# First stage of a spectral attention kernel: GpSimd normalises tokens before it multiplies the attention's column weights, and the DMA queue follows

## The chip, the cores and the metric

The kernel runs on one core of a Trainium2 chip. The metric is the time of one execution in microseconds (us). Three runs of the kernel before took 486.02, 487.41 and 488.27 us; the median is 487.41 us. Five engines work side by side and meet through semaphores: TensorE (PE) multiplies matrices, VectorE (DVE), ScalarE (ACT) and GpSimd (POOL) work on tiles in on-chip memory, and SyncE (SP) mostly issues transfers (DMAs). ACT and POOL can issue transfers from their own queues too.

## The reference, cut to what matters

The input x is 4 x 32 tokens, each an image of 128 x 128. The layer first normalises each image row (`_ln_c`), then runs an attention whose key, query, value and projection are spectral convolutions with 16 heads, then a two-layer spectral mixer, and last a recurrent network over the rows.

```python
x = x + conv(_ln_c(x), ...)          # rows of 128 values: mean 0, variance 1
t = _to_tokens(x)
t = t + ffn(_ln_t(t), W, V, gamma, beta)

# inside conv
k = fno_layer(tokens_norm, key_w, key_skip_w, ...)       # spectral, 16 heads
q = fno_layer(tokens_norm, query_w, query_skip_w, ...)
v = fno_layer(tokens_norm, value_w, value_skip_w, ...)
dprod = softmax(einsum('bhtd,bhsd->bhts', q, k) / scale)
attn = einsum('bhts,bhsd->bhtd', dprod, v)
attn = fno_layer(attn, proj_w, proj_skip_w, ...)         # value and projection
```

Value and projection act on the same spectral modes. The kernel multiplies their weights once into one table `wy` (16 heads x 16 columns x 3 parts x 32 rows of modes) and applies it to the tokens' spectra.

## The kernel before, in words

The first stage works on `x_h` (the tile BIG2), which holds image rows on the partitions and 128 tokens of 128 values along the free side. It is loaded in XC = 8 chunks of 16 tokens. For each chunk

- DVE takes the moments (`ln_moments`, line 1156, 16 instructions and four small ones), asks ACT for a square root (line 942), and forms scale and shift (`ln_coefs`, lines 1175 and 1176; semaphore `ln_coef`);
- POOL normalises the first LN_POOL[c] tokens (line 566) and ACT the rest (line 979), in place;
- PE multiplies each normalised token with a Fourier basis (line 620), four tokens to a PSUM bank, in the order P1_AT: ACT's tokens of the chunk first, then POOL's;
- ACT moves the banks to `rs` in the tile BIG1 (`spectra`, line 389), one chunk behind its own normalising;
- SP writes the normalised chunk to DRAM (`xn_rows`, line 480), since its place in BIG2 is used again.

LN_POOL is 4, 8 and then six times 12, which makes 84 tokens for POOL and 44 for ACT. PE also multiplies `rs` with itself (`gram`), in pieces of work between the chunks 2 to 5 and after the stage.

Before it normalises, POOL copies four weight planes (line 534, waited for by PE's first transposes) and forms `wy` in 15 instructions (lines 551 to 561), the first of which waits for ACT's two instructions of line 968 (`wy_skip`). ACT runs those behind its queue of 27 small loads (lines 958 to 965). SP writes `wy` to DRAM (line 483) and reads it back as `wr`, each head's row repeated on 32 partitions: 16 transfers of 192 KB (line 489). They are spread between the writes of chunks 4 to 7 by WR_AFTER, and land in the first 6144 columns of BIG2, which chunks 0 to 2 held.

After the stage, PE forms inner products over the spectra (`rx`, eight banks moved by ACT and DVE), and the modes `ts` of every token. SP repeats `ts` as `xrep` on the partitions (line 496, 16 transfers of 192 KB, tile to tile), loads the mixer's weights (line 500) and reads the normalised tokens back from DRAM in another layout, `x_t` (line 511). `x_t` lies in BIG1 over `rs`, so its transfers 0 and 1 wait for the first of four grams, 2 and 3 for the second, and so on; the last two wait for the fourth. DVE forms the scores and the softmax and then multiplies `xrep` with `wr` (`products`, line 1262, 32 instructions: two, then the softmax's normalising, then six, then 8 and 16). The first two wait for all 16 transfers of `wr` (`rep_w`) and for the first half of `xrep`, the next six for its second half (`rep_x_23`). PE applies the attention to the products (`attend`), between pieces of gram. The mixer begins when `x_t` is there.

The order on each engine and in each queue is that of the code; nothing is planned at run time.

Of the kernel before, what the change touches and what calls it, by code (L numbers as in the profile page):

```python
# [149 lines left out]
def metaformer(nc, t, out):  # L150
# [4 lines left out]
    with ctx:  # L155
# [366 lines left out]
        def _(pool):  # L522
# [13 lines left out]

            def lows(v):
                return v.rearrange("n w (q h) -> n w q h", h=8)[:, :, 0::3, :]

            def a(part):  # L540
                return w_val[:, :, 1:9, part].rearrange("n (k h) w -> n w k h", k=2)

            def b(part):
                return lows(w_proj[:, :, 1:1 + LW, part].rearrange("n h w -> n w h"))


            pool.wait_ge(S("wy_skip"), 1)
            for part, (p, q, op) in ((0, (0, 0, ALU.add)), (0, (1, 1, ALU.subtract)),
                                     (1, (0, 1, ALU.add)), (1, (1, 0, ALU.add))):
                o = lows(wy[:, 0:LW, 1 + part, :])  # L550
                link(pool.tensor_tensor(wtmp, b(p), a(q), ALU.mult))
                link(pool.tensor_tensor(o, o, wtmp, op))
            for part in range(2):
                o = lows(wy[:, 0:LW, 1 + part, :])
                link(pool.tensor_scalar(wtmp, a(part), ps, None, ALU.mult))
                link(pool.tensor_tensor(o, o, wtmp, ALU.add))

            wy_re, wy_im = wy[:, :, 1, :], wy[:, :, 2, :]
            link(pool.tensor_tensor(wy[:, :, 0, :], wy_re, wy_im, ALU.add))
# [987 lines left out]
```

## Time and profile before

| what | value |
|---|---|
| median of three runs | 487.41 us |
| span of the profiled execution | 486.8 us |
| PE busy | 359.3 us (74%) |
| DVE busy | 349.1 us (72%) |
| ACT busy | 263.1 us (54%) |
| POOL busy | 232.1 us (48%) |
| mean granted clock of PE | 0.904 |
| bytes moved by DMA | 50.93 MB, 105 GB/s on average |

The profiled execution's own time is its span; 0.6 us lie between it and the median. The busy shares are averages over stages that have different limits, so the stage that the change touches, the first 140 us, has to be read by itself: in the chain of waits (what the end depended on, followed back), in the order of time on each engine, and in stretches of time with the transfer rates.

### The profile page before, as it was taken

How to read it: one execution, taken by the hardware profiler on the slowest of the kernel's cores; microseconds unless marked ns; L12 is line 12 of the kernel's file. 1: busy time of each engine (PE TensorE's matmuls, PEld its weight loads, DVE VectorE, ACT ScalarE, POOL GpSimd, SP SyncE). 2: the span in 40 equal slices, each digit the busy share in tenths (PEclk: the TensorE clock that was granted, in tenths of full speed). 3: DMA queues.
4: the chain of work that ended last, by engine and by line, in shares of the span. 5: the costliest groups of instructions: out<-in, count | busy, mean ns of one | idle time of the engine just before them, and what ended most of it. 6: DMA issues, size and time to landing. Idle time of an engine off the chain costs nothing.

```text
span 486.8 us, 7018 instructions
## 1 busy us (share of the span) xinstructions
PE 359.3 (74%) x2385; PEld 280.4 (58%) x2385; DVE 349.1 (72%) x954; ACT 263.1 (54%) x530; POOL 232.1 (48%) x268
## 2 busy tenths in 40 slices
PE   0169989998949999999916748666775557996790
PEld 0169967784529998799915724233332244664790
DVE  3689312798969645999586577777887369799790
ACT  0778743520227963555312147888889858597000
POOL 1499950000039949986111957666660599000000
PEclk9989999999969998999966957999989959799795
DMA  8999894998130007979980000000000000000599
GB/s 211 266 302 304 224 305 124 205 294 373 41 133 1 1 1 88 130 92 175 111 100 2 1 0 1 2 0 0 1 1 0 1 0 0 1 2 0 146 286 260
DMA packets 60692, 50.93 MB, mean 105 GB/s; under 512 B 4512, under 2 KB 54096, under 8 KB 59632
## 3 DMA queue, kind: packets, MB, share of 16 engines
q1 hardware_dynamic: 40928, 41.79, 29.4%
q0 software_dynamic: 16512, 8.39, 14.1%
q10 hardware_dynamic: 3216, 0.30, 0.6%
q8 instruction: 19, 0.31, 0.3%
q14 instruction: 17, 0.14, 0.1%
HBM read 30.45 MB, written 16.88 MB: 97 GB/s over the span
## 4 chain that ended last, share of the span: by engine, by line
DVE 38%; PE 27%; POOL 14%; ACT 9%; issue 5%; ACTq 3%; DMA 1%; DVEq 0%; SPq 0%
PE PS L620 24%; POOL BIG L566 8%; DVE PS L1468 7%; DVE BIG L1262 4%; DVE SML L1156 4%; PE PS L624 3%; DVE BIG L1436 3%; POOL BIG L606 3%; ACT BIG L1083 2%; POOL BIG L601 2%; DVE BIG L1519 2%; ACT SML L389 2%; DVE SML L1450 2%; ACTq L965 2%; DMA BIG<-xn_rows 1%
## 5 line engine op out<-in xcount | busy, mean ns | idle before, releaser
L620 PE MATMUL PS<-CST,BIG 128*128 128x128 f32 (+6 forms) x994 | 130.5, 327 | 22.6 <-ACT BIG L979 9.9
L620 PEld LDWEIGHTS PS<-CST,BIG 128*128 128x128 f32 (+1 forms) x994 | 115.4, 203 | 41.8 <-issue 13.7
L624 PE MATMUL PS<-CST,BIG 128*128 128x128 f32 (+1 forms) x326 | 53.9, 313 | 52.2 <-ACT SML L389 24.3
L624 PEld LDWEIGHTS PS<-CST,BIG 128*128 128x128 f32 (+1 forms) x326 | 43.9, 187 | 73.9 <-issue 54.6
L579 POOL COPY BIG<-BIG 128x512 f32<-128x512 f32 x24 | 30.2, 1307 | 74.8 <-DMA BIG<-xn_rows 71.2
L1156 DVE BATCH_NORM_STATS2 SML<-BIG 128x6 f32<-128x128 f32 x256 | 53.4, 279 | 6.1 <-DMA BIG<-in_x 4.8
L620 PE MATMUL PS<-BIG 128*128 128x128 f32 (+2 forms) x450 | 53.5, 368 | 2.6 <-DVE BIG L1262 2.1
L601 POOL TENSOR_TENSOR BIG<-BIG,SML 128x512 f32<-128x512 f32 x32 | 33.2, 1038 | 45.7 <-DVE SML L1176 27.9
L620 PE MATMUL PS<-BIG,SML 128*128 128x256 f32 (+3 forms) x214 | 49.1, 440 | 5.8 <-ACT BIG L1104 5.8
L389 ACT ACTIVATE BIG<-PS 128x512 f32<-128x512 f32 (+3 forms) x59 | 33.0, 571 | 33.7 <-PE PS L620 26.9
L1083 ACT ACTIVATE BIG<-BIG,SML 128x128 f32<-128x128 f32 x112 | 46.1, 486 | 3.9 <-DVE SML L1176 3.9
L620 PEld LDWEIGHTS PS<-BIG 128*128 128x128 f32 (+2 forms) x450 | 40.6, 168 | 13.0 <-issue 8.2
L1468 DVE SCALAR_TENSOR_TENSOR PS<-BIG,SML,PS 128x256 f32<-128x256 f32 x92 | 41.6, 489 | 6.1 <-PE PS L620 6.0
L620 PEld LDWEIGHTS PS<-BIG,SML 128*128 128x128 f32 (+1 forms) x214 | 32.0, 189 | 21.1 <-ACT BIG L1104 5.9
L620 PE MATMUL PS<-SML 128*128 128x512 f32 (+2 forms) x74 | 40.1, 635 | 4.9 <-DVE SML L1493 4.3
L585 POOL TENSOR_TENSOR BIG<-BIG,SML 128x512 f32<-128x512 f32 x32 | 39.5, 2477 | 7.3 <-ACT BIG L1048 7.3
L606 POOL TENSOR_TENSOR BIG<-BIG 128x512 f32<-128x512 f32 x32 | 40.6, 1270 | 0.0
L613 POOL TENSOR_TENSOR BIG<-BIG,SML 128x512 f32<-128x512 f32 x32 | 31.9, 1036 | 17.3 <-ACT BIG L1083 17.3
L566 POOL TENSOR_SCALAR BIG<-BIG,SML 128x128 f32<-128x128 f32 x84 | 37.0, 449 | 0.0
L1115 ACT ACTIVATE BIG<-PS,SML 128x256 f32<-128x256 f32 x80 | 35.5, 473 | 0.8 <-DVE PS L1468 0.4
L1436 DVE TENSOR_TENSOR BIG<-BIG,PS 128x512 f32<-128x512 f32 x32 | 21.7, 678 | 18.5 <-POOL BIG L606 16.9
L389 ACT ACTIVATE SML<-PS 128x512 f32<-128x512 f32 x32 | 34.5, 1077 | 0.0
(210 smaller groups left out, 513.1 us busy)
## 6 DMA issues: line engine op xcount, KB each, us to landing
xn_rows<-BIG SPq DMA_DIRECT2D x8, 1024.0 KB, 7.5
BIG<-xn_rows SPq DMA_DIRECT2D x8, 1024.0 KB, 9.1
BIG<-in_x POOLq DMA_DIRECT2D x8, 1024.0 KB, 11.1
out_x<-BIG SPq DMA_DIRECT2D x32, 256.0 KB, 3.6
BIG<-wy_rows SPq DMA_DIRECT2D x16, 192.0 KB, 5.4
BIG<-BIG SPq DMA_DIRECT2D x16, 192.0 KB, 4.0
BIG<-in_L_conv_mixer_w SPq DMA_DIRECT2D x2, 544.0 KB, 6.5
CST<-in_const SPq DMA_DIRECT2D x1, 547.5 KB, 8.8
```

What stands on the lines that cost most here:

```text
L389: return e.activation(o, i, ACT.Copy) if e is scalar_engine else e.tensor_copy(o, i)
L566: last = pool.tensor_scalar(x_h[:, n, :], x_h[:, n, :], ln_r[:, n:n + 1], ln_b[:, n:n + 1], ALU.mult, ALU.add)
L585: pool.tensor_tensor(m1[:, v, :], a0[:, v, :], kap[:, v].unsqueeze(2).to_broadcast([128, 4, W]), ALU.mult).then_inc(S("ka0"), 1)
L601: pool.tensor_tensor(m1[:, v, :], m1[:, v, :], bet[:, v].unsqueeze(2).to_broadcast([128, 4, W]), ALU.mult).then_inc(S("bm1"), 1)
L606: pool.tensor_tensor(a0[:, v, :], a0[:, v, :], m1[:, v, :], ALU.add).then_inc(S("xm"), 1)
L620: return pe.matmul(o, l, rhs, start=start, stop=stop, **k)
L624: return pe.matmul(o, i, ident[0:n, 0:n], is_transpose=True, start=True, stop=True)
L1083: last = act.activation(m1[:, n, :], a0[:, n, :], ACT.Identity, scale=ln_r[:, n:n + 1], bias=ln_b[:, n:n + 1])
L1115: act.activation(at(y_s, g, i * 2 + (j0 + dj)), sums(g, dj), ACT.Sigmoid, bias=s("bb")).then_inc(S("state"), 1)
L1156: last = dve.bn_stats(ln_st[:, c % 2, row, :], src[:, XR * c + row, :])
L1436: TT(v, v, halves(4 + g % 4), ALU.add).then_inc(S("x1"), 1)
L1468: STT(sums(b, dj), wx_step[:, b, :, bass.ds(j, 1), :], s("bs"), sums(b, dj), ALU.mult, ALU.add).then_inc(S("vy_wx"), 1)
```

## The change

It has four parts.

1. Eight of ACT's small loads (one value each, repeated on 128 partitions) are issued by POOL, at its start (POOL_LOADS). DVE waits for both groups.
2. POOL normalises all its tokens first and then forms `wy`. LN_POOL becomes 8, 8, five times 12, and 8: again 84 tokens. ACT's two instructions for `wy_skip` move from its start to chunk 3 of its loop, and ACT loads the table with the square root at the start.
3. SP writes the eight chunks to DRAM, then `wy`, and then reads `wr` in one piece of 16 transfers. WR_AFTER is gone.
4. In BIG2 the tiles change places: `rx` and the `u` tiles now lie over the first tokens' columns, `wr` over those of tokens 80 to 127, and the products from column 0. The waits for the chunks' writes are grouped to match (`xn_0_1`, `xn_2_4`, `xn_5_7`).

```diff
-LN_POOL = [4, 8] + 6 * [12]
+LN_POOL = [8, 8, 12, 12, 12, 12, 12, 8]
-WR_AFTER = [0, 0, 0, 0, 5, 10, 13, 16]
-XN_OUT = 4 * ["xn_0_3"] + 2 * ["xn_4_5"] + 2 * ["xn_6_7"]
+XN_OUT = 2 * ["xn_0_1"] + 3 * ["xn_2_4"] + 3 * ["xn_5_7"]
+POOL_LOADS = SCALARS[:8]
...
-        rx = BIG2[:, 8192:12288].rearrange("f (j t) -> f j t", t=NT)
+        rx = BIG2[:, 0:4096].rearrange("f (j t) -> f j t", t=NT)
...
-            (BIG2, 12288), (BIG2, 14336), (BIG2, 6144), (BIG3, 2144))]
+            (BIG2, 4096), (BIG2, 6144), (BIG2, 8192), (BIG3, 2144))]
-        wr = BIG2[:, 0:6144].rearrange("p (g w k h) -> p g w k h", g=4, k=3, h=MH)
+        wr = BIG2[:, 10240:16384].rearrange("p (g w k h) -> p g w k h", g=4, k=3, h=MH)
-        PROD_AT = [(BIG2, 6144 + 1536 * k) for k in range(6)] + [(BIG3, 10336), (BIG3, 2144)]
+        PROD_AT = [(BIG2, 1536 * k) for k in range(6)] + [(BIG3, 10336), (BIG3, 2144)]
...
@@ sync: for c in range(XC), after the chunk's write
-                if c == 2:
-                    sp.wait_ge(S("wy3"), 2)
-                    sp.dma_start(wy_rows, ...).then_inc(S("wy_out"), 16)
-                if c == 4:
-                    sp.wait_ge(S("wy_out"), 16)
-                    sp.wait_ge(S("rs_filled"), 48 // P1_T)
-                    sp.wait_ge(S("xn_0_3"), 64)
-                for n in range(wr_next, WR_AFTER[c]):
-                    sp.dma_start(wr[...], wy_rows[n:n + 1, :].to_broadcast(...)).then_inc(S("rep_w"), 16)
+            sp.wait_ge(S("wy3"), 2)
+            sp.dma_start(wy_rows, ...).then_inc(S("wy_out"), 16)
+            sp.wait_ge(S("wy_out"), 16)
+            sp.wait_ge(S("rs_filled"), P1_N)
+            sp.wait_ge(S("xn_5_7"), 48)
+            for n in range(NH):
+                sp.dma_start(wr[...], wy_rows[n:n + 1, :].to_broadcast(...)).then_inc(S("rep_w"), 16)
...
@@ gpsimd
+            for name in POOL_LOADS:
+                a, n = ROW_AT[name]
+                pool.dma_start(PRM[:, a:a + n], flat(t[name]).to_broadcast([128, n])).then_inc(S("prm_pool"), 16)
...
@@ scalar
             for name, (a, n) in ROW_AT.items():
-                if n <= NH:
+                if n <= NH and name not in POOL_LOADS:
...
-            act.wait_ge(S("w_in"), 16 * 6)
-            for part in range(2):
-                last = act.activation(wy[:, :, 1 + part, :], ..., ACT.Copy, scale=wcp[:, 1952:1953])
-            last.then_inc(S("wy_skip"), 1)
+            act.wait_ge(S("basis_in"), 16)
+            load_table(ACT.Sqrt)
...
                 if c:
                     spectra(c - 1)
+                if c == 3:
+                    act.wait_ge(S("w_in"), 16 * 6)
+                    for part in range(2):
+                        last = act.activation(wy[:, :, 1 + part, :], ..., ACT.Copy, scale=wcp[:, 1952:1953])
+                    last.then_inc(S("wy_skip"), 1)
...
@@ vector
-            dve.wait_ge(S("prm"), 16 * (len(ROW_AT) - 2))
+            dve.wait_ge(S("prm"), 16 * (len(ROW_AT) - 2 - len(POOL_LOADS)))
+            dve.wait_ge(S("prm_pool"), 16 * len(POOL_LOADS))
...
-            dve.wait_ge(S("xn_0_3"), 64)
-            dve.wait_ge(S("xn_6_7"), 32)
+            dve.wait_ge(S("xn_2_4"), 48)
```

On SP, the queue from the first chunk's write on, before. `xn_rows` is the normalised input in DRAM, `wy_rows` the weights there, BIG<-wy_rows the load of `wr`, BIG<-BIG that of `xrep`:

```order
L480 DMA xn_rows<-BIG 128x16x128 [waits ln_pool,ln_act] x3
L483 DMA wy_rows<-BIG 16x1536 [waits wy3]
L480 DMA xn_rows<-BIG 128x16x128 [waits ln_pool,ln_act] x2
L489 DMA BIG<-wy_rows 32x1536 [waits xn_0_3,rs_filled,wy_out]
L489 DMA BIG<-wy_rows 32x1536 x4
L480 DMA xn_rows<-BIG 128x16x128 [waits ln_pool,ln_act]
L489 DMA BIG<-wy_rows 32x1536 x5
L480 DMA xn_rows<-BIG 128x16x128 [waits ln_pool,ln_act]
L489 DMA BIG<-wy_rows 32x1536 x3
L480 DMA xn_rows<-BIG 128x16x128 [waits ln_pool,ln_act]
L489 DMA BIG<-wy_rows 32x1536 x3
L496 DMA BIG<-BIG 32x1536 [waits ts]
```

The same place on SP in the changed kernel:

```order
L479 DMA xn_rows<-BIG 128x16x128 [waits ln_pool,ln_act] x8
L481 DMA wy_rows<-BIG 16x1536 [waits wy3]
L486 DMA BIG<-wy_rows 32x1536 [waits xn_5_7,rs_filled,wy_out]
L486 DMA BIG<-wy_rows 32x1536 x15
L492 DMA BIG<-BIG 32x1536 [waits ts]
```

The write of `wy` has moved from behind three chunks to behind all eight, and the 16 loads of `wr` stand together, directly ahead of the 16 of `xrep`.

On POOL, the end of the forming of `wy` and the beginning of the normalising (TENSOR_SCALAR, waiting for `ln_coef`), before:

```order
L556 TENSOR_TENSOR BIG<-BIG 16x8x2x8 [waits pool_seq]
L559 TENSOR_TENSOR BIG<-BIG 16x16x32 [waits pool_seq]
L560 TENSOR_SCALAR BIG<-BIG 16x16x32 [waits pool_seq]
L561 TENSOR_TENSOR BIG<-BIG 16x16x32
L566 TENSOR_SCALAR BIG<-BIG,SML 128x128 [waits ln_coef]
L566 TENSOR_SCALAR BIG<-BIG,SML 128x128 x3
L566 TENSOR_SCALAR BIG<-BIG,SML 128x128 [waits ln_coef]
L566 TENSOR_SCALAR BIG<-BIG,SML 128x128 x7
```

And in the changed kernel, where the last two loads and the four copies stand directly ahead of the normalising:

```order
L529 DMA BIG<-in_L_conv_mixer_norm_b 128x1
L529 DMA BIG<-in_L_conv_mixer_norm_g 128x1
L534 COPY SML<-BIG 16x128 [waits w_in]
L534 COPY SML<-BIG 16x128 x3
L540 ISA
L540 TENSOR_SCALAR BIG<-BIG,SML 128x128 [waits ln_coef]
L540 TENSOR_SCALAR BIG<-BIG,SML 128x128 x7
L540 TENSOR_SCALAR BIG<-BIG,SML 128x128 [waits ln_coef]
L540 TENSOR_SCALAR BIG<-BIG,SML 128x128 x7
```

The 15 instructions for `wy` now follow the 84 of the normalising, and the first chunk has eight tokens on POOL in place of four.

## Rows read from the trace of the kernel before

**Rows 1.** Chain of waits, 0 to 160 us: start, length, engine, tile and line

```profile
16.03 2.36 ACT BIG L968 x2
...
18.46 0.64 POOL BIG L551
...
30.63 36.56 POOL BIG L566 x83
...
126.29 4.81 PE PS L620 x40
...
131.49 6.89 DMA BIG<-xn_rows
```

**Rows 2.** Order of time on DVE: start, length, line, operation, idle time before

```profile
16.98 0.17 DVE L1169 SCALAR_TENSOR_TENSOR SML<-SML 128x16 f32<-128x16 f32 x1
20.45 0.25 DVE L1175 RECIPROCAL SML<-SML 128x16 f32<-128x16 f32 x1 [3.30 <-ACT SML L942]
...
36.98 3.19 DVE L1156 BATCH_NORM_STATS2 SML<-BIG 128x6 f32<-128x128 f32 x16
...
41.37 3.19 DVE L1156 BATCH_NORM_STATS2 SML<-BIG 128x6 f32<-128x128 f32 x16
```

**Rows 3.** Order of time on DVE, 96 to 103 us

```profile
98.46 1.82 DVE L1262 TENSOR_TENSOR BIG<-BIG 128x768 f32<-128x768 f32 x2
...
101.93 1.83 DVE L1262 TENSOR_TENSOR BIG<-BIG 128x768 f32<-128x768 f32 x2
```

**Rows 4.** Order of time on PE, 40 to 60 us

```profile
48.85 3.74 PE L620 MATMUL PS<-CST,BIG 128*128 128x128 f32 x32
52.43 1.95 PE L620 MATMUL PS<-BIG 128*128 128x128 f32 x16
```

**Rows 5.** Order of time on ACT, 8 to 30 us and 66 to 72 us

```profile
7.52 0.52 ACTq L965 DMA_DIRECT2D BIG<-in_L_conv_norm_b  x1
...
20.95 4.74 ACT L979 ACTIVATE BIG<-BIG,SML 128x128 f32<-128x128 f32 x12 [0.53 <-DVE SML L1176]
...
68.42 0.60 ACT L389 ACTIVATE BIG<-PS 128x512 f32<-128x512 f32 x1 [1.12 <-PE PS L620]
```

**Rows 6.** Order of time on POOL and on PE, 8 to 14 us

```profile
9.18 1.39 POOL L534 COPY SML<-BIG 16x128 f32<-16x128 f32 x4 [8.73 <-DMA BIG<-in_L_conv_proj_skip_w]
...
11.60 1.20 PE L624 MATMUL PS<-CST,SML 16*128 16x16 f32 x6 [11.60 <-DMA SML<-in_L_ffn_beta]
```

**Rows 7.** Line 591, POOL's transfers: durations in ns, least, median and most

```profile
L591 POOL DMA_DIRECT2D BIG<-in_x x8: 2083/2618/3910, 184.0 to 245.9; - x8
```

**Rows 8.** The page's transfers: KB each, median us from issue to landing

```profile
BIG<-BIG SPq DMA_DIRECT2D x16, 192.0 KB, 4.0
...
wy_rows<-BIG SPq DMA_DIRECT2D x1, 96.0 KB, 6.6
BIG<-in_L_conv_proj_w ACTq DMA_DIRECT2D x1, 68.0 KB, 3.0
```

**Rows 9.** Order of time on SP's queue, 30 to 105 us

```profile
41.14 4.02 SPq L483 DMA_DIRECT2D wy_rows<-BIG  x1
...
84.27 14.12 SPq L496 DMA_DIRECT2D BIG<-BIG  x16
```

**Rows 10.** Stretches: length, busy us (instructions) by engine, PE's clock, DMA share, GB/s

```profile
57.00:60.00 3.00, 3.00 (x29) 3.00 (x28) 1.60 (x9) 2.61 (x6) 3.00 (x8) 1.00 1.02 218
65.00:68.00 3.00, 2.03 (x15) 1.74 (x15) 0.00 (x0) 1.19 (x2) 2.32 (x7) 1.00 0.99 220
71.00:73.00 2.00, 2.00 (x14) 0.58 (x10) 0.92 (x2) 0.60 (x1) 0.00 (x0) 1.00 1.01 244
85.50:100.50 15.00, 14.80 (x128) 11.62 (x127) 12.48 (x16) 6.76 (x19) 0.00 (x0) 1.00 0.99 210
105.00:120.00 15.00, 13.76 (x113) 7.32 (x112) 12.85 (x20) 1.62 (x3) 0.00 (x0) 1.00 1.01 423
```

**Rows 11.** Stretches of the same view, for the clock and a first byte

```profile
28.00:32.00 4.00, 0.14 (x1) 0.00 (x0) 3.85 (x20) 4.00 (x11) 3.99 (x7) 0.96 1.05 289
32.00:35.00 3.00, 2.99 (x14) 2.99 (x15) 2.98 (x16) 1.17 (x4) 3.00 (x8) 0.50 1.06 297
...
85.00:86.00 1.00, 1.00 (x11) 1.00 (x11) 0.97 (x2) 0.64 (x3) 0.00 (x0) 1.00 0.47 98
```

More of the change, by code:

```diff
@@ L500, in _ @@
                 sp.dma_start(PRM[:, a:a + n], flat(t[name]).to_broadcast([128, n])).then_inc(S("mixer_in"), 16)
-            sp.wait_ge(S("xn_0_3"), 64)
-            sp.wait_ge(S("xn_4_5"), 32)
-            sp.wait_ge(S("xn_6_7"), 32)
+            sp.wait_ge(S("xn_0_1"), 32)
+            sp.wait_ge(S("xn_2_4"), 48)
+            sp.wait_ge(S("xn_5_7"), 48)
             sp.wait_ge(S("rx_filled"), 8)
@@ L535, in _ @@
             last.then_inc(S("qk_c"), 1)
[L537 to L552, printed above, removed]
-            for part in range(2):
[L554 to L559, printed above, removed]
-            pool.tensor_scalar(wy[:, :, 0, :], wy[:, :, 0, :], -1.0, None, ALU.mult).then_inc(S("wy3"), 1)
-            pool.tensor_tensor(wy_im, wy_im, wy_re, ALU.subtract).then_inc(S("wy3"), 1)
             for c in range(XC):
@@ L569, in _, with lows, val, proj @@
                         last.then_inc(S("ln_pool"), 1)
+            def lows(v):
+                return v.rearrange("n w (q h) -> n w q h", h=8)[:, :, 0::3, :]
+            def val(part):
+                return w_val[:, :, 1:9, part].rearrange("n (k h) w -> n w k h", k=2)
+            def proj(part):
+                return lows(w_proj[:, :, 1:1 + LW, part].rearrange("n h w -> n w h"))
+            pool.wait_ge(S("wy_skip"), 1)
+            for part, (p, q, op) in ((0, (0, 0, ALU.add)), (0, (1, 1, ALU.subtract)),
+                                     (1, (0, 1, ALU.add)), (1, (1, 0, ALU.add))):
+                o = lows(wy[:, 0:LW, 1 + part, :])
+                link(pool.tensor_tensor(wtmp, proj(p), val(q), ALU.mult))
+                link(pool.tensor_tensor(o, o, wtmp, op))
+            for part in range(2):
+                o = lows(wy[:, 0:LW, 1 + part, :])
+                link(pool.tensor_scalar(wtmp, val(part), ps, None, ALU.mult))
+                link(pool.tensor_tensor(o, o, wtmp, ALU.add))
+            wy_re, wy_im = wy[:, :, 1, :], wy[:, :, 2, :]
+            link(pool.tensor_tensor(wy[:, :, 0, :], wy_re, wy_im, ALU.add))
+            pool.tensor_scalar(wy[:, :, 0, :], wy[:, :, 0, :], -1.0, None, ALU.mult).then_inc(S("wy3"), 1)
+            pool.tensor_tensor(wy_im, wy_im, wy_re, ALU.subtract).then_inc(S("wy3"), 1)
             pool.memset(gf, 0.0).then_inc(S("gf_zero"), 1)
@@ L963, in _ @@
             for name, (a, n) in ROW_AT.items():
-                if n <= NH:
+                if n <= NH and name not in POOL_LOADS:
                     act.dma_start(PRM[:, a:a + n], flat(t[name]).to_broadcast([128, n])).then_inc(S("prm"), 16)
-            act.wait_ge(S("w_in"), 16 * 6)
-            for part in range(2):
-                last = act.activation(wy[:, :, 1 + part, :], w_proj[:, :, 1:1 + MW, part].rearrange("n h w -> n w h"),
-                                      ACT.Copy, scale=wcp[:, 1952:1953])
-            last.then_inc(S("wy_skip"), 1)
+            act.wait_ge(S("basis_in"), 16)
+            load_table(ACT.Sqrt)
             act.wait_ge(S("wt_filled"), 1)
@@ L986, in _ @@
                     spectra(c - 1)
+                if c == 3:
+                    act.wait_ge(S("w_in"), 16 * 6)
+                    for part in range(2):
+                        last = act.activation(wy[:, :, 1 + part, :],
+                                              w_proj[:, :, 1:1 + MW, part].rearrange("n h w -> n w h"),
+                                              ACT.Copy, scale=wcp[:, 1952:1953])
+                    last.then_inc(S("wy_skip"), 1)
             spectra(XC - 1)
             root(s("s1"), s("rt"))
-            act.wait_ge(S("xn_4_5"), 32)
+            act.wait_ge(S("xn_0_1"), 32)
             empty(act, "rx", 0, 8, move_rx)
```

13 lines of the change are left out of this document (6 added, 7 removed).

## The prediction

> **What bounds the kernel now.** I read the chain of waits first. To 18.4 us it runs through ACT's queue of small loads and its two instructions for `wy_skip`, then through POOL's 15 for `wy`, and from 30.2 to 67.2 us through POOL's 84 normalisations without a gap: 83 of them in 36.56 us, 0.4405 us each [rows 1]. PE and ACT then finish the last tokens; ACT's last spectrum bank of the stage is moved at 69.02 us [rows 5]. So POOL bounds the first stage, and it begins late. Next I read DVE around 100 us. The chain goes there through the products, from the first two at 98.46 and the next six from 101.93 [rows 3] to PE's last gram, which ends at 131.1, and to the last two transfers of `x_t`, which land at 138.4, where the mixer begins [rows 1]. Last I read the transfer rates. That view decides this case: while `wr` or `xrep` is loaded, the DMA engines are busy all the time (share 0.99 to 1.02) though only 210 to 244 GB/s flow [rows 10]. In the kernel before, `wr` is loaded beside the first stage, where nobody waits for it, and `xrep` is there just before DVE asks for it.
>
> **Normalising.** It can begin once DVE has the coefficients. DVE ends the moments of chunk 1 at 17.15 us and then idles 3.30 us for ACT's root, which came late because of the loads, the two instructions for `wy_skip` and a table load [rows 2]. The eight loads that leave ACT (0.52 us the one shown [rows 5]), `wy_skip` (2.36 us [rows 1]) and the table load no longer stand ahead of the root, so the coefficients of chunk 0 come at 17.15 + 0.5 = 17.65. DVE's next two chunks take 4.39 us each, by the distance of two starts of its moments with POOL at work beside it (41.37 - 36.98 [rows 2]): chunk 2 is ready at 17.65 + 8.8 = 26.4. POOL does chunks 0 and 1 (8 tokens, 3.5 us each) in between. From there it has 68 tokens and no reason to wait: 68 x 0.4405 = 30.0, end at 56.4, which is 10.8 before the 67.2 of now.
>
> Neither PE nor ACT holds this up, since POOL needs only coefficients. A chunk costs PE 5.4 us with its piece of gram (48.85 to the gram's end at 54.38, overlapping a little [rows 4]) and POOL 5.3. ACT has 4 tokens a chunk at 0.4 us (12 in 4.74 [rows 5]), four banks of 0.60 [rows 5] and a root: 4.4 us. Its `wy_skip` in chunk 3 adds 2.36 once, and delays the coefficients of chunk 5 to about 40.5, while POOL wants them at 42.3. POOL reads `wy_skip` at 56.4. I cost that move at nothing; without this cover it would be 2.4. ACT has eight tokens in the first and last chunks, against 12 and 4 before; its last group is ready before POOL's. The stage ends about 10.7 us earlier, at 58.3.
>
> **The eight loads on POOL.** No row shows one. Two rows enclose it: the same load costs ACT's queue about 0.5 us [rows 5], and a far larger one costs POOL 2.08 to 3.91 [rows 7]. From 0.4 us on, eight take 4 us at the one and 17 at the other. POOL's four copies start at 9.18 in any case because of `w_in` [rows 6]. The copies (1.39), PE's transposes (1.20 [rows 6]), three evictions on ACT (0.7) and the root (0.3) have until 17.15, so POOL may be at its loads until 13.5, or 1.6 us for each. I take the lower row, since the load is the same one: cost 0. At 2.08 the cost is 3.5 (below). DVE's added wait for them ends before 24 us; it reads them after 55.
>
> **What is late next: `wr`.** The DMA queue is FIFO, and `wy` is now formed last.
> - POOL ends at 56.4; the 15 instructions take 18.46 to 30.19, 11.7 us [rows 1]: 68.1. With DVE idle beside them it may be 0.4 less.
> - SP writes `wy`, 96 KB. In the trace it took 6.6 us, of which 4.02 was an issue held up by the queue [rows 8, 9]; the rest and a free issue of 0.4 give 3.0. A load of 68 KB on a quiet queue took the same 3.0 [rows 8]. `wy` is in DRAM at 71.2. The bounds are 2.5 and 6.6; nothing else is in the queue, so I stay with 3.0, and with 3.6 for the late end, since 6.6 needs a held-up issue.
> - First bytes come 1.2 us after an issue (84.27 against a half-filled 85 to 86 [rows 9, 11]): 72.4.
> - `wr` is 16 x 32 x 6144 bytes = 3.15 MB. The three stretches with `wr` alone in flight mean 225 GB/s [rows 10]: 14.0 us, to 86.4.
> - `xrep` is as large and ran at 210 GB/s [rows 10]: 15.0, to 101.4. Its modes `ts` are there at 73.6, so it follows at once. 0.6 us for the last to land, given 4.0 from issue to landing [rows 8] and the last issue at 97.5: 102.0.
>
> DVE has its scores at 98.41 - 10.7 = 87.7. It then waits for all of `wr` and half of `xrep`, to 94.5, does two products and the softmax's normalising (3.47 us, 98.46 to 101.93 [rows 3]) to 98.0, and waits again, to 102.0. The kernel before started these six products at 101.93. From there every instruction of the chain is unchanged, so the whole gain of 10.7 us is spent waiting for a queue that was hidden before, and the sum is +0.1 us. The writes of the chunks (8.4 MB from 33 to about 62) are out of the way by then, and the waits on them are satisfied; the places in BIG2 change no duration.
>
> The profiled execution (486.8) becomes 486.9, and the median of 487.4 becomes 487.5.
>
> **The rule that speaks against this sum.** The rows show 210 GB/s for tile to tile at a share of 0.99 [rows 10]. The Trainium skill (DMA: Bandwidth & Descriptors, section Where 436 GB/s comes from) says that transfers within SBUF are bound by a fabric ceiling of 435 GB/s. By it `xrep` would take 7.2 us in place of 15.0, and the trace disagrees.
>
> **Rivals.** *A, the repeated loads are quick once they stand together.* `x_t` ran at 423 GB/s [rows 10], so the engines can do more; if the 210 to 244 come from mixing with other traffic, 6.3 MB take 14.9 us, all is there at 88, DVE is the bound and the gain is 98.46 - 87.7 = 10.7: 476.7. At 290 GB/s it would be 21.7, at 94.7 with the landing, and 7 us gained: 480. Against it: `xrep` was alone in its 15 us, and the share was full. 12%.
> *B, POOL is late with its loads (the slower side).* At 2.08 us each they end at 17.0, the copies at 18.4, the root at 20.6, the first coefficients at 21.1 in place of 17.65. All behind shifts by 3.5: 105.5, or 491.0. It decides from 1.6 us a load. For it: POOL's own row; against: that row is of 1 MB. 12%.
> *C, the clock.* PE idles from about 93, when its grams are done, to 98. After such a gap (28.1 to 32.0) its granted clock was 0.50, the lower level of 1.2 GHz, for 3 us [rows 11]. PE's steps on the chain behind 102 are some 7 us of attention, transposes and gram; a part of them slowed costs 1 to 3 us: 489.5. 6%.
>
> **How the numbers follow.** The sum has 70%. Its own bounds: early ends of all terms (55.9, 11.3, 2.5, 1.2, `wr` at 244 and `xrep` at 215 GB/s: 12.9 and 14.6, 0.5) give 98.9, 3 us faster, 484.5; late ends (57.4, 11.9, 3.6, 1.4, 15.0 and 15.5, 0.7) give 105.5, 491.0. I take 484.5 to 491.5 as the range, which leaves most of A and a part of B and C out. Half a per cent, 2.4 us, is what a measurement can tell from none. Of the 70, 6 lie beyond it on the fast side and 12 on the slow; A gives 12 to faster; B gives 10 to slower and 2 to same; C gives 3 and 3. Faster 18, same 57, slower 25.
>
> **What would show it.** Right: the last normalisation near 56.4; `wy_rows` written near 68; DMA share about 1.0 at some 215 GB/s from 72 to 101; DVE idle for about 7 us before its first two products and 4 before the next six, released by DMAs; six products from 102. Wrong: DVE not idle there; a rate over 260 GB/s while `wr` loads; POOL's loads ending after 13.5; the last normalisation after 58; PE at 0.5 behind 102.

## The result and the profile after

The changed kernel takes 490.26 us in the median of 12 runs (488.89 to 491.68), beside 487.4 us (486.01 to 496.38) of the kernel before: a ratio of 1.0063, with a 95% interval of 1.0046 to 1.0080. It is 0.6% slower, 3.1 us by the interval's middle. The profiled spans are 489.0 and 486.8 us at mean granted clocks of 0.908 and 0.904. The ratios, here and below, use only executions in the faster of the chip's two states, so they need not be the quotient of the medians.

The chain of waits of the changed kernel answers to [rows 1]. Columns are start, length, engine, tile and line:

```profile
2.65 13.71 DMA BIG<-in_x
16.39 3.21 DVE SML L1160 x16
...
29.71 29.84 POOL BIG L540 x68
...
71.23 2.24 DMA wy_rows<-BIG
...
91.36 13.92 DMA BIG<-BIG
105.38 5.30 DVE BIG L1267 x6
...
129.74 4.81 PE PS L620 x40
134.93 6.94 DMA BIG<-xn_rows
```

The chain now starts with the loads of `x`. POOL's 68 normalisations without a gap, `wy`, its write and `xrep` follow as forecast, but all of it about 3.4 us later than in the sum: the six products start at 105.38, against 102.0 in the sum and 101.93 before [rows 3], and the last pieces of `x_t` land at 141.87, against 138.4 before.

The order of time on DVE (start, length, line, operation, idle time before and what ended it) answers to [rows 2] and [rows 3]:

```profile
11.52 3.19 DVE L1160 BATCH_NORM_STATS2 SML<-BIG 128x6 f32<-128x128 f32 x16 [7.34 <-DMA BIG<-in_x]
...
16.39 3.19 DVE L1160 BATCH_NORM_STATS2 SML<-BIG 128x6 f32<-128x128 f32 x16 [0.94 <-DMA BIG<-in_x]
...
98.19 1.83 DVE L1267 TENSOR_TENSOR BIG<-BIG 128x768 f32<-128x768 f32 x2 [6.36 <-DMA BIG<-BIG]
...
105.38 5.30 DVE L1267 TENSOR_TENSOR BIG<-BIG 128x768 f32<-128x768 f32 x6 [3.75 <-DMA BIG<-BIG]
```

The waits of 6.36 and 3.75 us are the new ones, on `xrep` behind `wr`. The first two rows hold the rest of the loss. In the kernel before, the same two chunks start 2.6 and 3.2 us earlier:

```profile
8.94 3.19 DVE L1156 BATCH_NORM_STATS2 SML<-BIG 128x6 f32<-128x128 f32 x16 [4.41 <-DMA BIG<-in_x]
13.22 3.19 DVE L1156 BATCH_NORM_STATS2 SML<-BIG 128x6 f32<-128x128 f32 x16 [0.35 <-DMA BIG<-in_x]
```

POOL's order of time shows the moved loads, the first and the last of eight, and then the copies of [rows 6] and its first normalisations:

```profile
1.26 0.74 POOL L529 DMA_DIRECT2D BIG<-in_L_conv_norm_g  x1 [0.81 <-POOLq L1541]
...
5.19 0.57 POOL L529 DMA_DIRECT2D BIG<-in_L_conv_mixer_norm_g  x1
12.12 1.40 POOL L534 COPY SML<-BIG 16x128 f32<-16x128 f32 x4 [6.37 <-DMA BIG<-in_L_conv_proj_skip_w]
20.82 3.49 POOL L540 TENSOR_SCALAR BIG<-BIG,SML 128x128 f32<-128x128 f32 x8 [7.31 <-DVE SML L1180]
```

POOL is done with its loads by 5.8 us and then waits 6.37 us for a weight that came at 9.18 before. ACT's queue feels the loads too. Its issue at 3.54 us took 0.44 us before and takes 1.71 now:

```profile
3.54 1.71 ACTq L959 DMA_DIRECT2D SML<-in_L_ffn_W  x1
```

Two views of the same 3 us (length, then busy time of each engine, PE's clock, DMA share, GB/s), first of the kernel before:

```profile
3.00:6.00 3.00, 0.00 (x0) 0.00 (x0) 0.37 (x1) 0.00 (x0) 0.00 (x0) 1.00 0.92 251
```

And of the changed one, with the stretches that answer to [rows 10] and [rows 11]:

```profile
3.00:6.00 3.00, 0.00 (x0) 0.00 (x0) 0.37 (x1) 0.00 (x0) 2.75 (x6) 1.00 0.53 144
76.00:90.00 14.00, 13.80 (x119) 10.61 (x118) 10.43 (x17) 7.72 (x23) 0.00 (x0) 1.00 1.01 219
88.00:103.00 15.00, 10.67 (x93) 9.25 (x86) 5.43 (x8) 1.24 (x3) 0.00 (x0) 0.98 1.02 220
103.50:105.00 1.50, 1.50 (x9) 1.50 (x8) 0.00 (x0) 0.98 (x2) 0.00 (x0) 0.50 0.95 229
184.50:194.50 10.00, 9.17 (x84) 8.92 (x84) 4.77 (x8) 3.41 (x7) 9.69 (x11) 1.00 0.59 72
```

While POOL issues, the DMA engines move 144 GB/s in place of 251, and their busy share is 0.53 in place of 0.92, so they are not full but wait for work. From 76 to 103 us they are busy without a break at 220 GB/s. SP's queue (start, length, line, tile) gives the transfers' starts:

```profile
73.48 7.28 SPq L486 DMA_DIRECT2D BIG<-wy_rows  x16
80.80 11.15 SPq L492 DMA_DIRECT2D BIG<-BIG  x16
```

### The profile page after: what moved, and what is told of

Its sections match the earlier page's. It is cut to its first block, busy times and chain, and to the rows that moved or that the text cites. A ratio compares the mean times of both kernels' runs of the same rounds, so it can differ in the third digit from the quotient of the medians.

```text
span 489.0 us, 7018 instructions
## 1 busy us (share of the span) xinstructions
PE 359.6 (74%) x2385; PEld 279.7 (57%) x2385; DVE 349.5 (71%) x954; ACT 261.3 (53%) x530; POOL 236.4 (48%) x276
## 4 chain that ended last, share of the span: by engine, by line
DVE 35%; PE 26%; POOL 13%; DMA 8%; ACT 7%; issue 5%; SPq 4%; DVEq 0%; ACTq 0%
PE PS L620 22%; DVE PS L1473 7%; POOL BIG L540 6%; DVE SML L1160 5%; DVE BIG L1267 4%; PE PS L624 4%; DMA BIG<-BIG 3%; DMA BIG<-in_x 3%; ACT BIG L1087 3%; DVE BIG L1441 2%; ACT SML L389 2%; SPq L492 2%; POOL BIG L606 2%; DVE BIG L1524 2%; POOL BIG L601 2%
## 5 line engine op out<-in xcount | busy, mean ns | idle before, releaser
L620 PE MATMUL PS<-CST,BIG 128*128 128x128 f32 (+6 forms) x994 | 126.2, 319 | 14.1 <-ACT BIG L976 5.0
L620 PEld LDWEIGHTS PS<-CST,BIG 128*128 128x128 f32 (+1 forms) x994 | 111.8, 198 | 32.8 <-issue 11.9
L624 PE MATMUL PS<-CST,BIG 128*128 128x128 f32 (+1 forms) x326 | 55.1, 318 | 55.3 <-ACT SML L389 23.9
L624 PEld LDWEIGHTS PS<-CST,BIG 128*128 128x128 f32 (+1 forms) x326 | 44.6, 189 | 77.8 <-issue 52.5
L620 PE MATMUL PS<-BIG 128*128 128x128 f32 (+2 forms) x450 | 55.5, 373 | 5.6 <-DVE BIG L1267 5.2
L620 PEld LDWEIGHTS PS<-BIG 128*128 128x128 f32 (+2 forms) x450 | 42.2, 173 | 16.5 <-issue 8.4
L389 ACT ACTIVATE BIG<-PS 128x512 f32<-128x512 f32 (+3 forms) x59 | 32.0, 568 | 26.7 <-PE PS L620 19.6
L620 PE MATMUL PS<-SML 128*128 128x512 f32 (+2 forms) x74 | 41.2, 651 | 4.8 <-DVE SML L1498 4.2
L620 PEld LDWEIGHTS PS<-BIG,SML 128*128 128x128 f32 (+1 forms) x214 | 32.2, 190 | 21.2 <-ACT BIG L1108 5.9
L613 POOL TENSOR_TENSOR BIG<-BIG,SML 128x512 f32<-128x512 f32 x32 | 31.9, 1039 | 17.3 <-ACT BIG L1087 17.3
L1267 DVE TENSOR_TENSOR BIG<-BIG 128x768 f32<-128x768 f32 x32 | 28.1, 952 | 10.1 <-DMA BIG<-BIG 10.1
```

What stands on the lines that cost most here:

```text
L389: return e.activation(o, i, ACT.Copy) if e is scalar_engine else e.tensor_copy(o, i)
L620: return pe.matmul(o, l, rhs, start=start, stop=stop, **k)
L624: return pe.matmul(o, i, ident[0:n, 0:n], is_transpose=True, start=True, stop=True)
L1267: TT(prod(4 * hg + b)[:, w], xrep[:, b, w], wr[:, hg, w], ALU.mult).then_inc(S("prod"), 1)
```

## The experiments

The start of the six products is called T; it was 101.93 before ([rows 3] shows two of the six, where its window ends) and 105.38 after. Each T is read from the one profiled execution of its kernel. "The changed kernel" is the base of a diff unless it says otherwise.

### e1: the eight loads back on ACT's queue

```diff
-POOL_LOADS = SCALARS[:8]
+POOL_LOADS = []
```

> The changed kernel with its first part alone undone: all 27 small loads on ACT again. Theory S (start): the 3 us by which the change was later than my sum come from POOL issuing eight loads from 1.3 us on, while the first chunks of x load. Then x's chunk 1 is there near 13.2 us in place of 16.4, the last normalisation ends near 56.4 in place of 59.5, the six products start near 102.2 in place of 105.4, and the time is about 487.3 us. Rival Q (queue): the 3 us lie in the repeated loads, which move slower or land later than I took them; then the six products stay near 105 and the time near 490. Rival N: the start was late by chance; then this kernel and the changed one agree.

It took 487.92 us (12 runs, ratio to the kernel before 0.9978, 0.9951 to 1.0005); span 487.3. On DVE:

```profile
8.57 3.19 DVE L1160 BATCH_NORM_STATS2 SML<-BIG 128x6 f32<-128x128 f32 x16 [4.35 <-DMA BIG<-in_x]
13.58 3.19 DVE L1160 BATCH_NORM_STATS2 SML<-BIG 128x6 f32<-128x128 f32 x16 [1.07 <-DMA BIG<-in_x]
...
102.66 5.30 DVE L1267 TENSOR_TENSOR BIG<-BIG 128x768 f32<-128x768 f32 x6 [3.92 <-DMA BIG<-BIG]
```

Chunk 1 is back at 13.58, POOL's 68 start at 26.87, T is 102.66. The loads' move costs 2.7 us of T. In time it costs 2.3 us by the two medians and 4 us by the two ratios to the kernel before (1.0063 and 0.9978), since the two kernels were timed in different sessions. Without it, the remaining three parts of the change are worth nothing, as the sum had for the whole.

### e2: the kernel before with the loads' move alone

```diff
+POOL_LOADS = SCALARS[:8]
...
+            for name in POOL_LOADS:
+                a, n = ROW_AT[name]
+                pool.dma_start(PRM[:, a:a + n], ...).then_inc(S("prm_pool"), 16)
...
-                if n <= NH:
+                if n <= NH and name not in POOL_LOADS:
```

> The kernel before with the first part of the change alone: eight small loads on POOL, all else as before. Theory S: x's chunk 1 and the weights come 3 us late here too (16.4 and 12.1 us), but ACT's queue is 4 us shorter, so its two instructions for wy_skip end near 14.5 in place of 18.4, POOL's chain of 15 and 84 instructions starts and ends 3.9 us earlier (63.3), and as wr is loaded beside the stage, all of it arrives: six products near 98, time about 483.5 us. Under rival N chunk 1 comes at 13.2, with the same time.

486.66 us (12 runs, 0.9963, 0.9929 to 0.9998); T = 99.48, span 482.5. The moments are late here too (10.76 and 15.61), and `w_in` comes at 11.01. But the kernel before does not need `x` early: POOL has `wy` to form first, and that begins when ACT's queue lets `wy_skip` go, 16.07 against 18.46 [rows 1]. So the same move gains 2.5 us of T in one order and loses 2.7 in the other. T was expected at 98, so the gain fell 1.5 us short, and the time missed 483.5 by 3.2. The weights are not the reason, since they are there at 11.01 and ACT's table load ahead of `wy_skip` starts only at 12.31, directly behind its queue. The queue itself became shorter by 2.4 us and not by 4, mainly because two of its issues were held up (they took 0.44 and 0.45 us before):

```profile
3.54 2.07 ACTq L964 DMA_DIRECT2D SML<-in_L_ffn_W  x1
5.64 0.85 ACTq L965 DMA_DIRECT2D SML<-in_L_ffn_V  x1
```

### e3: `wy` formed by DVE, POOL only normalises (on e1)

```diff
+            dve.wait_ge(S("wy_skip"), 1)
...
-                link(pool.tensor_tensor(wtmp, proj(p), val(q), ALU.mult))
-                link(pool.tensor_tensor(o, o, wtmp, op))
+                link(dve.tensor_tensor(wtmp, proj(p), val(q), ALU.mult))
+                link(dve.tensor_tensor(o, o, wtmp, op))
```

All 15 instructions move so, to behind the last coefficients on DVE.

> The changed kernel with all small loads on ACT and the 15 instructions for wy on DVE, right after its last coefficients, in place of POOL behind its normalising. Queue theory: what ate the gain of the first stage is that wy is formed last. wy is ready near 56, it is written to DRAM by 62 and wr is loaded by 77, xrep by 92, when DVE has its scores at 88 and its first two products and the softmax done at 91. The gain of the stage arrives: six products near 92.5, time about 478 us. Rival: if DMA is the bound however it is ordered, or DVE and POOL hold each other up in the 15 instructions, the products start at 97 or later and the time stays over 482.

486.18 us (12 runs, 0.9924, 0.9889 to 0.9960). T is 98.16, where 92.5 was expected; it is the rival of the expectation (97 or later, a time over 482) that came. Two steps missed: POOL's 68 took 32.20 us with DVE's new instructions beside them (29.68 in e1), and the loads of `wr` left at 66.35 only, behind the write of `wy` (issue held 3.2 us at 58.97) and those of the last chunks. Of the 3.8 us by which T is earlier than in the kernel before, 3.7 arrive in the time by the ratio and 1.9 by the medians (486.18 against 488.12 in the same session). None arrives in the profiled execution, which is a long one (488.73 us, span 486.9), and this window shows what took them:

```profile
175.90:195.90 20.00, 18.64 (x109) 17.54 (x110) 7.58 (x17) 6.88 (x11) 19.59 (x19) 0.66 0.57 69
```

PE's granted clock is 0.66 there (0.91 in the kernel before), and the stretch from the Gelu table load to the second Sqrt load takes 62.6 us against 57.9. The twelve executions of this one kernel took from 482.37 us, at a mean clock of 0.913, to 491.63, at 0.895, so the clock differs between executions of the same code.

### e4: half of `wr`

```diff
-            for n in range(NH):
+            for n in range(NH // 2):
...
-            dve.wait_ge(S("rep_w"), 16 * NH)
+            dve.wait_ge(S("rep_w"), 16 * NH // 2)
```

> The changed kernel with the loads of wr for heads 8 to 15 left out (8 transfers of 192 KB in place of 16; the products for those heads then use whatever lies there). Queue theory: everything behind them is 7 us earlier, since wr and xrep go one after the other at some 220 GB/s and DVE waits for the end of both; six products near 98.4, time about 483.3 us. Rival: if DVE does not really wait for bytes but for something fixed behind the write of wy, the time stays near 490.

482.61 us (6 runs, 0.9852, 0.9813 to 0.9891). The six products:

```profile
97.26 5.30 DVE L1267 TENSOR_TENSOR BIG<-BIG 128x768 f32<-128x768 f32 x6 [3.23 <-DMA BIG<-BIG]
```

From the first load of `wr` to T it is 24.8 us (72.42 to 97.26) in place of 31.9: eight loads are worth 7.1, as their 1.57 MB at 220 GB/s are. The rest of the 8.1 us by which T is earlier comes from a first load 1.1 us sooner. So the queue sets T.

### e5: a version that starts `wr` sooner

Diff against the kernel before, whose loads and places in BIG2 stay:

```diff
-LN_POOL = [4, 8] + 6 * [12]
+LN_POOL = [8, 8, 12, 12, 12, 12, 12, 8]
-WR_AFTER = [0, 0, 0, 0, 5, 10, 13, 16]
+WR_AFTER = 7 * [0] + [16]
...
-                if c == 2:
+                if c == 6:
                     sp.wait_ge(S("wy3"), 2)
...
-                if c == 4:
+                if c == 7:
```

`wy` is formed on DVE as in e3, `wy_skip` on ACT in chunk 3 as in the changed kernel.

> The layout and the small loads of the kernel before, POOL normalising from the first coefficients, the 15 instructions for wy on DVE as in the run before this, and wy written behind chunk 6, wr (16 transfers, over the first tokens' columns) straight behind chunk 7. Queue theory: wr no longer waits for the last chunks' writes to land, so its bytes flow from about 61.5 in place of 67.6 us, all of wr and xrep is there by about 92.5, and the six products start near 92.5 in place of 98.2: 5.5 us sooner than in the run with wy on DVE, about 12.9 sooner than in the changed kernel. Rival: PE's granted clock takes it back. In the run with wy on DVE the products started 3.8 us before those of the kernel before and the span was the same, with the clock at 0.50 for 10 us behind 181; if such a dip belongs to the earlier schedule, the time stays near 486, if not it is near 479.

480.54 us (6 runs, 479.65 to 486.04; 0.9872, 0.9815 to 0.9928), span 478.4: faster than both kernels. DVE's order of time has no wait on a DMA before either group of products:

```profile
90.71 1.82 DVE L1267 TENSOR_TENSOR BIG<-BIG 128x768 f32<-128x768 f32 x2
...
94.19 5.30 DVE L1267 TENSOR_TENSOR BIG<-BIG 128x768 f32<-128x768 f32 x6
```

POOL's row again shows what DVE's work beside it costs, 32.52 us for the 68:

```profile
26.78 32.52 POOL L540 TENSOR_SCALAR BIG<-BIG,SML 128x128 f32<-128x128 f32 x68 [0.92 <-DVE SML L1153]
```

`wr` leaves at 62.83, 10.7 us before that of the changed kernel, and `xrep` at 76.53. The 7.7 us that the first stage saves here (DVE reads its variances at 60.86, against 68.61 before) arrive at T (94.19), and 8.4 in the span. T stays 1.7 us behind the 92.5 expected, since DVE itself is ready no sooner.

### e6 and e7: where the eight loads stand

e6 has POOL issue them behind its copies; e7 has ACT issue them first of its queue.

```diff
-            for name in POOL_LOADS:
-                a, n = ROW_AT[name]
-                pool.dma_start(PRM[:, a:a + n], ...).then_inc(S("prm_pool"), 16)
...
             last.then_inc(S("qk_c"), 1)
+            for name in POOL_LOADS:
+                a, n = ROW_AT[name]
+                pool.dma_start(PRM[:, a:a + n], ...).then_inc(S("prm_pool"), 16)
```

> The changed kernel with POOL's eight loads issued behind its four copies, near 11 to 15 us, and not from 1.3 us on. If it is the moment that matters (small loads beside x's first chunks), chunk 1 of x is there near 13.4 and the six products start near 102.6, time near 487.8, as with all loads on ACT. If it is POOL's queue whenever it is used, the chunks behind (2 and 3) come late in its place; these have 1 us to spare, and the products start near 104 to 105. If neither, chunk 1 still comes near 16.

487.63 us (12 runs, 1.0021, 0.9984 to 1.0059). The moments of the first four chunks in e6, with the loads issued from 9.95 to 14.4:

```profile
8.08 3.19 DVE L1159 BATCH_NORM_STATS2 SML<-BIG 128x6 f32<-128x128 f32 x16 [3.74 <-DMA BIG<-in_x]
...
12.29 3.19 DVE L1159 BATCH_NORM_STATS2 SML<-BIG 128x6 f32<-128x128 f32 x16 [0.28 <-DMA BIG<-in_x]
...
17.40 3.19 DVE L1159 BATCH_NORM_STATS2 SML<-BIG 128x6 f32<-128x128 f32 x16 [0.81 <-DMA BIG<-in_x]
...
23.34 3.19 DVE L1159 BATCH_NORM_STATS2 SML<-BIG 128x6 f32<-128x128 f32 x16 [1.63 <-DMA BIG<-in_x]
```

The delay has moved with the loads: chunks 0 and 1 are early, chunks 2 and 3 wait. T is 103.05.

e7, where ACT has the diff:

```diff
-POOL_LOADS = SCALARS[:8]
+POOL_LOADS = []
...
+            for name in SCALARS[:8]:
+                a, n = ROW_AT[name]
+                act.dma_start(PRM[:, a:a + n], ...).then_inc(S("prm"), 16)
...
-                if n <= NH and name not in POOL_LOADS:
+                if n <= NH and name not in SCALARS[:8]:
```

> The changed kernel with the same eight small loads issued at the same time as there, from the start, but by ACT, ahead of its other loads. If it is POOL's queue that makes x's first chunks late, the moments of chunk 0 start near 8.6 us and of chunk 1 near 13.5, the six products near 102.7 and the time is near 488. If it is small loads that run beside the first chunks, whoever issues them, they start near 11 and 16 as in the changed kernel, and the time is near 490.

490.89 us (10 runs, 1.0060, 1.0024 to 1.0095), T = 105.65. It fits neither expectation cleanly. The moments are 1 us late (9.82 and 14.46), less than with POOL's loads, but the weights are very late (POOL's copies at 14.88), so ACT's root comes at 19.89 and the first coefficients at 20.7 all the same. Its view of the 3 us from above:

```profile
3.00:6.00 3.00, 0.00 (x0) 0.00 (x0) 0.37 (x1) 0.00 (x0) 0.00 (x0) 1.00 0.45 139
```

The traffic falls as with POOL's loads, to 139 GB/s, though POOL issues nothing here. So eight small loads ahead of `x` cost something on either queue, and POOL's way of issuing cannot be the whole cause. The moments of chunk 1 start at 14.46 here, at 14.86 to 16.40 over the seven kernels in which POOL issues the loads at its start, and at 12.29 to 13.58 over the six with no such loads that early. What in the DMA engines does that, I did not find out.

### e8 to e11: the rate of the repeated loads

e8 loads `wr` in four transfers of 128 partitions:

```diff
-            for n in range(NH):
-                sp.dma_start(wr[TB * (n % HG):..., n // HG]..., wy_rows[n:n + 1, :].to_broadcast([TB, 3 * MW * MH]))
+            for g in range(4):
+                src = wy_rows[HG * g:HG * g + HG, :].unsqueeze(1).to_broadcast([HG, TB, 3 * MW * MH])
+                sp.dma_start(wr[:, g].rearrange("s w k h -> s (w k h)"), src).then_inc(S("rep_w"), 16)
...
-            dve.wait_ge(S("rep_w"), 16 * NH)
+            dve.wait_ge(S("rep_w"), 16 * 4)
```

> The changed kernel with wr loaded by 4 transfers that each write all 128 partitions (768 KB) in place of 16 that each write 32; the same bytes and rows. Theory P (ports): a transfer that writes 32 partitions reaches half of the memory's DMA ports, which is why wr and xrep flow at 220 GB/s and x_t, over 128 partitions, at 423. By the Trainium skill (SBUF: State Buffer, Door 1: The DMA port swizzle) 32 partitions lie on 8 of 16 ports, half of 435 GB/s. Then wr takes about 7.5 us in place of 14, the six products start near 98.9 and the time is near 484. Rival R (rows): the rate belongs to rows of 6 KB, each read 32 times from one place in DRAM; then wr stays at 220 GB/s, the products at 105 and the time at 490.

519.88 us (6 runs, 1.0665, 1.0621 to 1.0710), T = 135.33. Its windows, the first before `xrep` is issued:

```profile
74.00:76.00 2.00, 2.00 (x20) 2.00 (x19) 0.78 (x5) 2.00 (x8) 0.00 (x0) 1.00 0.25 80
76.00:90.00 14.00, 13.80 (x119) 10.61 (x118) 10.78 (x15) 6.51 (x20) 0.00 (x0) 1.00 0.31 102
```

The share is 0.25 and 0.31: most engines stand idle. So this run says nothing on width; it failed for another reason. The Trainium skill (DMA: Bandwidth & Descriptors, section Why a DMA increments its semaphore by 16 and not by 1) has the number of engines as the largest up to 16 that divides the slowest dimension of both sides; a source of 4 rows gives 4, a quarter, and the trace agrees with its 0.25.

e9 takes the heads in the order 0, 2, 1, 3, so that neighbouring transfers go to the lower and the upper half of the partitions:

```diff
-            for n in range(NH):
+            for n in (4 * g + k for g in range(4) for k in (0, 2, 1, 3)):
...
-                for n in range(HG):
+                for n in (0, 2, 1, 3):
```

> The changed kernel with the 16 transfers of wr and of xrep issued in the order of heads 0, 2, 1, 3 in each four, so that two that follow each other write partitions 0 to 31 and 64 to 95, on different halves of the ports, and no more 0 to 31 and 32 to 63. Theory P with engines that run ahead into the next transfer: two transfers share both halves, the rate rises over 260 GB/s, products near 100 and time near 485. If the engines keep in step, or under rival R, the rate stays at 220 and the time at 490.

488.38 us (12 runs, 485.89 to 493.15; 1.0037, 0.9995 to 1.0079), unclear in time. The rate is not:

```profile
75.00:87.00 12.00, 11.80 (x104) 9.99 (x106) 10.12 (x16) 7.88 (x24) 0.00 (x0) 1.00 1.02 245
87.00:101.00 14.00, 11.77 (x104) 10.20 (x97) 5.43 (x8) 2.19 (x3) 0.00 (x0) 1.00 1.02 247
```

246 GB/s in place of 220 for the same bytes: 28.9 us to T (101.60) in place of 31.9. The 260 of theory P was not reached.

e10 and e11 fill `wr` from the normalised tokens in DRAM, 128 different rows, so that neither a repeated source nor a small first dimension is in play. e10 keeps 16 transfers to 32 partitions, e11 makes 4 to 128. Both leave out the weights and first wait for the writes of all chunks.

```diff
-                sp.dma_start(wr[TB * (n % HG):..., n // HG]..., wy_rows[n:n + 1, :].to_broadcast([TB, 3 * MW * MH]))
+                rows, cols = slice(TB * (n % HG), TB * (n % HG) + TB), slice(1536 * (n // HG), 1536 * (n // HG) + 1536)
+                sp.dma_start(wr[rows, n // HG]..., xn_flat[rows, cols]).then_inc(S("rep_w"), 16)
```

> The changed kernel with wr filled from other data: 16 transfers to 32 partitions each, 6 KB a row, but each row from its own place in DRAM (the normalised tokens) and not the head's weights 32 times. It leaves out the weights. Theory P (a transfer to 32 partitions reaches half the ports): still 220 GB/s, six products near 105, time near 490. Rival R (the same place read again and again): the rate rises over 300 GB/s and the products start near 101.

489.48 us (10 runs, 1.0044, 1.0007 to 1.0082), 31.7 us from the first load to T:

```profile
75.00:85.00 10.00, 9.80 (x86) 8.92 (x88) 8.82 (x13) 7.20 (x21) 0.00 (x0) 1.00 1.02 224
```

The rate is that of `wr` from one row repeated, so reading one place again and again is not what limits it. e11:

```diff
+            for g in range(4):
+                sp.dma_start(wr[:, g]..., xn_flat[:, 1536 * g:1536 * g + 1536]).then_inc(S("rep_w"), 16)
...
+            dve.wait_ge(S("rep_w"), 16 * 4)
```

> As the run before it (wr from other data, each row from its own place), but in 4 transfers that write all 128 partitions, 6 KB a row. Both sides have 128 rows, so all 16 engines take part, and not 4 as in the wide run before. Theory P: over 380 GB/s, wr takes 7.5 us in place of 14, the six products start near 98.9, time near 484. Rival: rows of 6 KB are slow in themselves (x_t had 8 KB); then 220 GB/s and 490.

483.94 us (10 runs, 0.9922, 0.9884 to 0.9960):

```profile
74.00:80.00 6.00, 6.00 (x53) 5.81 (x53) 2.88 (x7) 4.29 (x14) 0.00 (x0) 1.00 0.91 338
76.00:81.00 5.00, 5.00 (x48) 5.00 (x47) 3.88 (x8) 3.81 (x14) 0.00 (x0) 1.00 1.03 424
```

The first window holds the start of the transfers, with a share of 0.91. Once they run, 424 GB/s flow for the same bytes (e10's window starts later and has no such loss), which is more than the 380 expected. In the same run `xrep`, still in transfers to 32 partitions, flows at 226 GB/s from 84 to 96 us. It is 26.2 us to T (73.51 to 99.68). The Trainium skill (SBUF — State Buffer, section Door 1: The DMA port swizzle) has partitions 0 to 63 on 8 of the 16 ports and 64 to 127 on the other 8; e9 (246), e10 (224) and e11 (424) agree with it.

e11 against e10 changes the size of a transfer (768 KB in place of 192) together with its partitions, and no run separates the two. e9 changes only which partitions follow each other and gains 26 GB/s, so the partitions count for something by themselves. The stores of the output, 256 KB each from all 128 partitions to DRAM, speak for them too. In the kernel before:

```profile
460.00:480.00 20.00, 13.71 (x95) 13.52 (x94) 14.90 (x25) 0.00 (x0) 0.00 (x0) 0.89 1.02 286
```

286 is above the 246 of e9 and far below 424, so the partitions are not the only thing that sets a rate.

### e12: e5 with four tokens fewer on POOL

```diff
-LN_POOL = [8, 8, 12, 12, 12, 12, 12, 8]
+LN_POOL = [8, 8, 12, 12, 12, 12, 8, 8]
```

> The kernel that wrote wy sooner and formed it on DVE, with four tokens of chunk 6 moved from POOL to ACT (LN_POOL 8, 8, 12, 12, 12, 12, 8, 8). There POOL ended its normalising at 59.2 and PE waited 1.58 us for it, so 1.5 us less are to be had: stage end near 59.7 in place of 61.2, six products near 92.7 in place of 94.2, if the DMA queue lets them, time near 479. Rival: xrep was landed only just before; then the products stay near 94 and the time at 480.5.

485.94 us (6 runs, 479.13 to 488.24; 0.9846, 0.9788 to 0.9904). DVE:

```profile
95.14 5.30 DVE L1267 TENSOR_TENSOR BIG<-BIG 128x768 f32<-128x768 f32 x6 [3.04 <-DMA BIG<-BIG]
```

DVE is ready 2 us sooner than in e5, but `wr` leaves at 62.79 as there, and `xrep`, issued over 14.2 us from 74.49, ends the wait. The queue bounds again. T is 1 us later than in e5, and the version shows no gain over it.

## Why the prediction was right in kind and short by 2.8 us

The forecast was 487.5 us, the time 490.26. It lies inside the range, but beyond the half per cent around no change, which had the greatest chance (57%); slower had 25%. The steps:

| step | sum | profile |
|---|---|---|
| POOL's loads, each | up to 1.6 free | 0.56 to 0.74 |
| first 68-token stretch starts | 26.4 | 29.71 |
| 68 normalisations | 30.0 | 29.84 |
| `wy`, 15 instructions | 11.7 | 11.7 |
| write of `wy` | 3.0 | 2.25 |
| first load of `wr` to T | 30.8 | 31.9 |
| T | 102.0 | 105.38 |

**The step that failed** is "I take the lower row, since the load is the same one: cost 0". Its reasoning asked how long POOL is held up, and on that it was right: the decision point was 1.6 us a load, and they took 0.6. It did not ask what the loads do to the transfers beside them. They run beside the chunks of `x` and the weights, which come 2.6 to 3.2 us later. In the kernel before, that would hide behind the forming of `wy`; the change takes this very cover away, since POOL now normalises first. e1 shows it (2.7 of T back), e2 that the old order bears it, e6 that the delay goes where the loads go, and e7 that it is not POOL's queue alone. How small loads slow their neighbours stays open.

**Rival B** was thus right in size (3.5 us, 491.0) and wrong in mechanism. Whoever saw the time alone would have called it confirmed.

**The queue** is as forecast: DVE idle for 6.36 and 3.75 us (7 and 4 were named), share 1.0, 220 GB/s. The stage ends 6.7 us sooner (DVE reads its variances at 61.89 against 68.61) and none of it arrives. The sum had 10.7, and late loads are not all that is missing: e1 reaches 59.09, or 9.5. POOL normalises up to 59.55 in the changed kernel, and PE, whose last two chunks run without a wait, needs to 61.66:

```profile
54.35 7.31 PE L620 MATMUL PS<-CST,BIG 128*128 128x128 f32 x64
```

"Neither PE nor ACT holds this up" was right for POOL, but not for the end of the stage. It costs T nothing here, because `wr` waits for `wy`.

e4 and e5 show both sides of the queue: fewer bytes or an earlier start give the microseconds back at once. The write of `wy` was 0.75 us shorter than in the sum. The repeated loads were 1.1 us longer, though their rate was not lower: 220 GB/s flowed, where the sum had 225 for `wr` and 210 for `xrep`. The whole stretch, in the changed kernel:

```profile
73.50:105.40 31.90, 27.37 (x222) 23.80 (x221) 15.59 (x25) 11.92 (x31) 0.00 (x0) 0.95 0.99 220
```

That is 7.0 MB, and `wr` and `xrep` hold 6.3. Something of the loads issued behind them, from 91.99 us, has thus probably flowed ahead of their last bytes. That this is the 1.1 us is an inference; no run tests it.

**Rival A** fell: together and alone on the engines the loads do not speed up. It is not the repeated source that holds their rate (e10). In transfers to all 128 partitions, four times as large, the same bytes flow nearly twice as fast (e11). The trace of before could not show either.

**Rival C** came, with no price. PE stands idle for 4.33 us to 101.68, and its granted clock is 0.50 (1.2 GHz) from 103.5 to 105, but DVE's products were the last to be waited for, and the gram keeps its 4.81 us.

**What was given back.** T is 3.45 us later, `x_t` 3.49, the span only 2.2. ACT's table loads mark the mixer stage, before and then after:

```profile
179.52 1.28 ACT L931 ACT_TABLE_LOAD   x1
237.44 1.28 ACT L931 ACT_TABLE_LOAD   x1
```

```profile
182.49 1.28 ACT L931 ACT_TABLE_LOAD   x1
239.31 1.28 ACT L931 ACT_TABLE_LOAD   x1
```

The first of them is 2.97 us later, so 0.5 us goes ahead of the stage. The stage itself took 57.9 us and takes 56.8. In the window from 184.5 to 194.5 PE's clock is 1.00 (above), and in the kernel before:

```profile
184.50:194.50 10.00, 9.17 (x66) 8.51 (x66) 5.49 (x13) 3.86 (x6) 10.00 (x10) 0.83 0.87 107
```

e1 has 0.83 as well and e5 1.00. One profile stands for each kernel, and e3's executions show that the clock differs between executions of the same code. What decides it stays open, so the 1.1 us are seen and not explained.

## What to carry to other kernels

When work is reordered, ask what the old order was hiding: here `wy` first covered both a late `x` and the whole load of `wr`, and the new order lost both covers. Cost a moved DMA by what it slows in flight as well as by its issue. Where a queue sets the end, what helped here was fewer bytes (e4), an earlier first issue (e5) or wider and larger transfers (e11), and a stage made faster ahead of it gains nothing.

## What the runs showed of the hardware

- Loads of 0.5 KB issued by POOL took 0.56 to 0.74 us each to issue, where its 1 MB ones took 2.08 to 3.91 [rows 7]. Beside them all DMA traffic fell from 251 to 144 GB/s (3 to 6 us, share 0.92 to 0.53). With the same loads on ACT's queue it was 139.
- Transfers of 192 KB to 32 partitions ran at 210 to 224 GB/s over stretches of 10 us and more with every engine busy ([rows 10] and e10), with alternating halves at 246 (e9), and those of 768 KB to 128 partitions at 424 (e11): a DMA share of 1.0 does not mean full bandwidth.
- DVE's 15 instructions for `wy` beside POOL's normalisations made the 68 take 32.2 to 32.5 us in place of 29.7 (e3 and e5 against e1).
- PE's granted clock in the middle of the mixer stage was between 0.66 and 1.00 over 20 us (e3 and the changed kernel), in kernels whose code differs only ahead of that stage; with 0.66 the stage took 4.7 us more than in the kernel before.
